# Value blocks of the image normalised before their projection, and the first two images' statistics chains in another order

## The reference, cut to what matters

```python
x = x + gate * _gn(x)        # gate: one number per image and channel
# gate = sigmoid(w_deform . sampled(pooled) + b), pooled = mean over pixels of _gn(x),
# sampled at i + k - 1 + conv3(pooled), clipped, with linear interpolation
y = _gn(x)                   # of the new x
value = conv1x1(y, v_w, v_b)                     # 64 channels
keyf, query = proj(y, k...), proj(y, q...)       # two 1x1 convs with batch norm and relu
# 27 neighbours of each pixel: 3 x 3 at distances 1, 2 and 4; outside the image: zero
sim = softmax(sum_c(query * unfold(keyf)), axis=neighbours)
x = x + conv1x1(sum(sim * unfold(value)), w_w, w_b)
```

## Time and profile before

| | before |
|---|---|
| median of 3 runs | 1502.79 us (1501.54 to 1503.92) |
| profiled execution, its own time | 1504.14 us |
| its span | 1502.4 us |
| TensorE busy | 1452.5 us, 97% |
| VectorE busy | 1240.1 us, 83% |
| ScalarE busy | 1163.9 us, 77% |
| GpSimd busy | 824.5 us, 55% |
| chain that ended last | PE 94%, POOL 2%, issue 2%, DVE 1%, ACT 1% |
| load of an image, 1568 KB | 6.6 us from issue to landing (median) |

### The profile page before, as it was taken

The page is one execution under the profiler, slowest core; times in us unless marked ns, Lnnn a source line. Parts: engine busy times, 40 slices in busy tenths (PEclk is TensorE's granted clock), DMA queues, the critical chain, the costliest instruction groups (busy, mean ns, idle before and its releaser), DMA issues.

```text
span 1502.4 us, 35364 instructions
## 1 busy us (share of the span) xinstructions
PE 1452.5 (97%) x9159; PEld 1189.1 (79%) x9159; DVE 1240.1 (83%) x4631; ACT 1163.9 (77%) x3044; POOL 824.5 (55%) x2313
## 2 busy tenths in 40 slices
PE   1799999999999999999999999999999999999998
PEld 0588888888888888888888888888888888888886
DVE  6488888888888888888888888888888888888876
ACT  2487787887787887787887787887787887787876
POOL 5645565654565654565655565654565655565620
PEclk9999999999999999999999999999999999999999
DMA  2244544454543454544454543454544455543344
GB/s 92 77 123 149 166 111 119 145 166 149 165 116 115 145 166 149 165 106 125 145 166 149 167 115 115 144 166 150 166 107 124 144 166 150 163 123 112 101 122 142
DMA packets 104708, 205.97 MB, mean 137 GB/s; under 512 B 13632, under 2 KB 83776, under 8 KB 96448
## 3 DMA queue, kind: packets, MB, share of 16 engines
q1 hardware_dynamic: 103632, 203.49, 45.8%
q10 hardware_dynamic: 880, 0.23, 0.1%
HBM read 51.62 MB, written 51.38 MB: 69 GB/s over the span
## 4 chain that ended last, share of the span: by engine, by line
PE 94%; POOL 2%; issue 2%; DVE 1%; ACT 1%; ACTq 0%; POOLq 0%; DVEq 0%
PE ps_s L432 23%; PE ps_o L465 20%; PE ps_v L505 12%; PE ps_t L444 11%; PE ps_p L487 11%; PE ps_p L482 11%; PE ps_o L470 3%; PE ps_v L521 1%; PE ps_v L533 1%; PE ps_v L525 1%; POOL hats L767 0%; PE ps_v L528 0%; ACTq L585 0%; POOL xb L836 0%; PE ps_v L532 0%
## 5 line engine op out<-in xcount | busy, mean ns | idle before, releaser
L597 ACT ACTIVATE e<-e,zmin 128x256 f32<-128x256 f32 x800 | 402.8, 503 | 125.0 <-DVE zmin L969 120.4
L969 DVE CUSTOM_DVE_ANT_0 e<-ps_s,mask 128x256 f32<-128x256 f32 x800 | 338.3, 423 | 175.4 <-PE ps_s L432 166.3
L465 PEld LDWEIGHTS ps_o<-eT,v 128*128 128x128 f32 x2688 | 380.3, 191 | 85.3 <-issue 81.6
L465 PE MATMUL ps_o<-eT,v 128*128 128x128 f32 x2688 | 433.4, 276 | 0.1
L432 PE MATMUL ps_s<-kk,qq 128*128 128x256 f32 x1408 | 425.2, 384 | 0.1
L444 PE MATMUL ps_t<-ident,e 128*128 128x128 f32 x1600 | 305.7, 273 | 0.0
L612 ACT ACTIVATE eT<-ps_t 128x512 f32<-128x512 f32 (+1 forms) x416 | 235.7, 567 | 78.2 <-PE ps_t L444 75.8
L444 PEld LDWEIGHTS ps_t<-ident,e 128*128 128x128 f32 x1600 | 225.2, 141 | 80.5 <-issue 0.2
L432 PEld LDWEIGHTS ps_s<-kk,qq 128*128 128x128 f32 x1408 | 223.6, 192 | 47.7 <-issue 41.2
L986 DVE SCALAR_TENSOR_TENSOR e<-e,rz,keep 128x256 f32<-128x256 f32 x480 | 246.0, 513 | 17.1
L505 PE MATMUL ps_v<-wvox,xb 128*128 128x128 f32 x1600 | 219.9, 278 | 0.9 <-DVE v L1007 0.8
(11 more groups left out here) (150 smaller groups left out, 1809.8 us busy)
## 6 DMA issues: line engine op xcount, KB each, us to landing
out_dram<-raw SPq DMA_DIRECT2D x32, 1568.0 KB, 5.7
raw<-in_x_dram SPq DMA_DIRECT2D x31, 1568.0 KB, 6.6
v<-v SPq DMA_DIRECT2D x192, 224.0 KB, 2.9
kk<-kk SPq DMA_DIRECT2D x192, 112.0 KB, 2.2
ksp<-kk SPq DMA_DIRECT2D x192, 64.0 KB, 2.1
v<-v_last SPq DMA_DIRECT2D x64, 128.0 KB, 2.9
kk<-kk SPq DMA_DIRECT2D x32, 224.0 KB, 2.9
v<-v_last SPq DMA_DIRECT2D x64, 96.0 KB, 2.7
```

What stands on the lines that cost most here:

```text
L465: last = nc.tensor.matmul(o[:, UPIX * (u - 1):UPIX * (u + 1)], v[:, s, u, :], eT[:, UPIX * (base + 2 * u - 1):UPIX * (base + 2 * u + 1)], ...
L597: nc.scalar.activation(e[:, i, :], e[:, i, :], ACT.Exp, bias=zmin[:, i:i + 1], scale=-1.0, accum_out=zs[:, i:i + 1]).then_inc(e_done.next( ...
L969: nc.vector.tensor_tensor_reduce(e[:, i, :], ps_s[(TILES * n.parity() + t) % 2][:, 0:KEYS], mask[:].rearrange("p s h a b -> p (s h a b)"), ...
```

## The change

- **Blocks normalised.** `spread` writes `xb` = raw * `Y_A` + `Y_B` with `tensor_scalar` (two scalars per partition) where it copied. The value matmuls take the constant `wvoT`, VectorE adds the constant `wobv`. `yb_row`, `wvox`, `bias`, the second matmul of c6 and step 16 of VectorE's chain go. `spread` of block 0 waits for p11.
- **Shorter chain steps.** Pairs of GpSimd steps become one with two scalars (rsqrt, `diag`, the new moments): p3 writes also `ROOT` = variance * rsqrt, and d7 computes `RG` = 1 / ((1 + EX) * ROOT), so p7 starts with the mean of the new x, and its moments are ready with the fourth step, not the seventh. GpSimd's chain has 32 counts (40 before), VectorE's 15 (16).
- **Image 0 and 1.** Image 0's hats: ScalarE also does three `Relu`, VectorE weighs and adds them (GpSimd's eight steps are only counted). d6 of image 0 moves from slot 25 to 22. Image 1's d6 to pw move later (25..32 to 29..34), its statistics to the slots behind image 0's d9. Image 0's first three strips of projections come 3, 3 and 2 slots earlier. The load of image 2 is issued 19 slots earlier.
- **Tables.** `mask_tables` becomes `distances` (slot 21), `crosses` (behind d7) and `mask_table` (behind image 1's `aggr`). The 19 memsets of `keep` and the wait for the zero fill move behind image 0's p3 (`borders`).
- **All images:** `queries` of strips 0, 2, 3 and 6 one slot later; TensorE's `hidden` no longer waits for `b1x`, ScalarE's does.
- **Dummy matmuls** of 384 columns into `ps_s[0]`: nine behind image 0's c3, five behind its c4.

```diff
+QUERIES_LATER = (0, 2, 3, 6)
+FIRST_UP = (3, 3, 2)
+CH_OF = {0: dict(CH, d6=22), 1: dict(CH, d6=29, a6=29, d7=30, p7=30, c4=31, d9=31, p11=33, pw=34)}
+STATS_1 = {4: (0,), 5: (1,), 6: (2,), 8: (3,), 10: (4,), 12: (5, 6)}
+AWAKE = {CH["c3"]: 9, CH["c4"]: 5}
...
-                        if t == LOAD and (n + 3).exists():
+                        if t == (LOAD if n.offset != -1 else 0) and (n + 3).exists():
...
-                                                    wvox[:, m.parity(), :], start=True, stop=True)
+                                                    wvoT[:], start=True, stop=True)
...
-                            nc.tensor.matmul(ps_v[:, 0:1], w1T[:], col(Y_B + m.parity()), start=True, stop=True)
-                            nc.tensor.matmul(ps_v[:, P:2 * P], yb_row[:], wvoT[:], start=True,
+                            nc.tensor.matmul(ps_v[:, 0:1], w1T[:], col(Y_B + m.parity()), start=True,
                                              stop=True).then_inc(cg.next(), 1)
...
+                    def awake(count):
+                        for _ in range(count):
+                            nc.tensor.matmul(ps_s[0][:, 0:TAPS * P], ident[:], band[:].rearrange("p a b -> p (a b)"),
+                                             start=True, stop=True)
...
+                                if rel == at + (2 if g in QUERIES_LATER else 1):
                                     queries(m, g)
...
+                                for k in range(TAPS) if m.offset == 0 else ():
+                                    act.wait_ge(ag.sem, ag.count(m, k + 1))
+                                    nc.scalar.activation(hats[:, k, 1, :], hats[:, k, 0, :], ACT.Relu, bias=ones[:, 0:1],
+                                                         scale=-1.0).then_inc(a_hats, 1)
...
-                                  lambda: gp.tensor_tensor(col(RG), col(R), col(GATE), ALU.mult),
-                                  lambda: gp.tensor_tensor(col(T0), col(RG), col(D), ALU.mult),
-                                  lambda: gp.tensor_tensor(moment(of_x1, MEAN), col(T0), moment(of_x, MEAN), ALU.add),
+                                  lambda: gp.tensor_scalar(moment(of_x1, MEAN), col(D), col(RG), moment(of_x, MEAN),
+                                                           ALU.mult, ALU.add),
...
-                                  lambda: gp.tensor_tensor(col(T0), a, a, ALU.mult),
-                                  lambda: gp.tensor_tensor(moment(of_x1, VAR), col(T0), moment(of_x, VAR), ALU.mult),
+                                  lambda: gp.tensor_scalar(moment(of_x1, VAR), moment(of_x, VAR), a, a, ALU.mult,
+                                                           ALU.mult),
...
-                                  lambda: gp.tensor_scalar(yb_row[:], ones[:], col(Y_B + i), None, ALU.mult),
-                                  lambda: gp.tensor_scalar(w1x[:, i, :], w1T[:], col(Y_A + i), None, ALU.mult),
-                                  lambda: gp.tensor_scalar(wvox[:, i, :], wvoT[:], col(Y_A + i), None, ALU.mult))
+                            steps(31, lambda: gp.tensor_scalar(w1x[:, i, :], w1T[:], col(Y_A + i), None, ALU.mult))
...
+                            gp.wait_ge(pg.sem, pg.count(m, 31))
...
-                            gp.tensor_copy(to[:, 0, 0:HALO, cs], rows[:, H - HALO:H, at])
-                            gp.tensor_copy(to[:, 0, HALO:SIDE, cs], rows[:, 0:HALO, at])
-                            last = gp.tensor_copy(to[:, 1:CHUNKS, :, cs], rows[:, HALO:H - HALO, at].rearrange(
-                                "p (n r) c -> p n r c", r=SIDE))
+                            for k, rs, src in ((0, slice(0, HALO), rows[:, H - HALO:H, at]),
+                                               (0, slice(HALO, SIDE), rows[:, 0:HALO, at]),
+                                               (slice(1, CHUNKS), slice(0, SIDE), rows[:, HALO:H - HALO, at].rearrange(
+                                                   "p (n r) c -> p n r c", r=SIDE))):
+                                last = gp.tensor_scalar(to[:, k, rs, cs], src, col(Y_A + m.parity()),
+                                                        col(Y_B + m.parity()), ALU.mult, ALU.add)
...
-                                                bias[:, m.parity(), :].unsqueeze(1).to_broadcast([P, last - first, P]),
+                                                wobv[:].unsqueeze(1).to_broadcast([P, last - first, P]),
...
+                        if at == ch(m)["p4"] and m.offset == 0:
+                            dve.wait_ge(pg.sem, pg.count(m, 9))
+                            dve.wait_ge(a_hats, 1)
+                            nc.vector.tensor_scalar(hat_sum[:], hats[:, 0, 1, :], wg_s[:, 9:10], None,
+                                                    ALU.mult).then_inc(pg.sem, 1)
...
-                            step(11, nc.vector.tensor_scalar(col(EX), col(EX), 1.0, None, ALU.add))
-                            step(12, nc.vector.reciprocal(col(GATE), col(EX)))
+                            step(11, nc.vector.scalar_tensor_tensor(col(EX), col(EX), 1.0, col(ROOT), ALU.add, ALU.mult))
+                            step(12, nc.vector.reciprocal(col(RG), col(EX)))
```

More of the change, by code:

```diff
@@ L57 @@
 PIECES = 4
[L59 to L63, removed]
+AWAKE = {CH["c3"]: 9, CH["c4"]: 5}
+CHAIN_READS = ((2, "d1"), (4, "d4"), (13, "d9"), (15, "d13"))
+N_DG, N_PG, N_CG, N_AG = 15, 32, 4, 4
 def half_tile(h):
@@ L146, in end_part, with g_slots, ch @@
         self.here = 0
+def g_slots(m):
+    return [at - (FIRST_UP[g] if m.offset == 0 and g < len(FIRST_UP) else 0) for g, at in enumerate(G_SLOT)]
+def ch(m):
+    return CH_OF.get(m.offset, CH)
 def lagged(n, t, lag):
@@ L712, in _, with borders @@
                     gp.memset(zs[:], 1.0).then_inc(g_zs, 1)
[L713 to L726 removed]
+                    def borders():
+                        gp.wait_ge(v_zero, 3)
+                        cut = 0
+                        for k, kind in enumerate(KINDS):
+                            parts = slice(0, HD)
+                            for part in kind:
+                                if part == "lower":
+                                    parts = slice(HD, P)
+                                    continue
+                                s_at, h_at, rs, cs = part
+                                gp.memset(keep[parts, k, :].rearrange("p (s h r c) -> p s h r c", s=2, h=2, c=SIDE)[
+                                    :, s_at, h_at, rs, cs], 0.0).then_inc(g_keep, 1)
+                                cut += 1
+                                gp.wait_ge(g_keep, cut)
+                        gp.wait_ge(a_zero, 3)
                     def chain(m, at):
@@ L842, in slot @@
                             chain(m, at)
+                        if n.offset == first + 1 and t == CH["p3"] + 1:
+                            borders()
                         for m, rel in items_at(n, t):
@@ L934, in tables @@
                         if t == CH["d4"] + 1:
[L935 removed]
+                            distances()
                         if t == CH["c1"]:
@@ L1015, in step @@
                             dve.wait_ge(dg.sem, dg.count(m, k))
-                        for u in STATS.get(at, ()):
+                        for u in (STATS_1 if m.offset == 1 else STATS).get(at, ()):
                             if u == (2 * (PIECES - 1) if m.offset == 0 else 0):
@@ L1065, in chain @@
                                                              bn_t[:, 0:1], ALU.add))
-                            step(16, nc.vector.tensor_tensor(bias[:, m.parity(), :], ps_v[:, P:2 * P], wobv[:],
-                                                             ALU.add))
                     def slot(n, t):
@@ L1071, in slot @@
                             tables(t)
+                        if n.offset == -1 and t == CH["d7"] - TILES + 1:
+                            crosses()
+                        if n.offset == -1 and t == CH["d13"] - TILES + 2:
+                            mask_table()
                         if n.exists():
```

149 lines of the change are left out of this document (72 added, 77 removed).

## The result

| | before | after |
|---|---|---|
| median of 4 runs each | 1502.2 us (1501.54 to 1503.92) | 1491.67 us (1490.16 to 1492.69) |
| ratio, 95% interval | | 0.9926 [0.9914, 0.9938] |
| profiled execution; its span | 1504.14; 1502.4 us | 1492.62; 1490.9 us |
| c6 of image 0, of image 1, of image 31 (start on TensorE) | 36.8, 81.4, 1433.1 us | 30.4, 70.7, 1420.9 us |
| one image, c6 to c6, median of the images from 1 on | 45.01 us | 44.97 us |

The change is a gain of 0.74%, 10.5 us, where 21.5 was forecast. The time is 6.2 us above the forecast's range (1478 to 1485.5) and 1.7 above the one for 8 in 10 (1490). The two places named in the prediction give the split at once: the period is 44.97, above the mark of 44.95 from which I called the steady part wrong, and the values of b = 4 come at 54.86, just inside the mark of 55.

A forecast was written before the change was run, and what follows sets the result against it. TensorE's queue was taken to bound the steady part, the statistics chains of images 0 and 1 the start. 1502.79 - 12.5 (start) - 9.0 (steady: -7.1 - 6.6 + 3.7 + 1.0) = 1481.3 us; range 1478 to 1485.5, 8 in 10 1475.5 to 1490.

The forecast's parts named there:

- c6's second matmul: TensorE's queue, steady part: removing this narrow matmul saves 0.23 us an image, -7.1 us over 31 images.
- c1: TensorE's weight load no longer waits for GpSimd's `of_x` once `bias` goes: -0.22 x 30 = -6.6 us; bounds 0 and -6.6.
- the cost at c4: Dearer GpSimd block writes, less a shorter p7, make TensorE wait 0.12 us an image: +3.7 us (0 to +18).
- a longer stop at c4: Rival: 0.3 to 0.6 us an image through contention of GpSimd with VectorE, 1487 to 1496 us; chance 0.12.
- a stop of 0.8 us and a time of 1502: Rival of about no change: six block writes 0.25 us dearer each, stop at c4 costing 25 us in all; chance 0.02.
- Queries: ScalarE's queries one slot later; strip 6 delays the next `hidden` by 0.03 us an image: +1.0 us.
- The start: Up to about 66 us, the statistics chains of images 0 and 1 shorten: -12.5 us (-8 to -15).
- Legs 1 and 2: Start, image 0: p1 2.2 us earlier, `Abs` ending at 20.0; then d6 at 22.7, 2.7 us after `Abs`.
- Leg 3: Start, d6 to c4 of image 0: 3.3 us, less 0.6 for p7, so c4 at 25.5.
- Leg 6: Start, `hidden` to image 1's `Abs`: 12.3 us, was 14.1, with TensorE at 2.4 GHz and three strips moved up; `Abs` at 42.6.
- The clock rival: TensorE's clock falls in the start: at 1.2 GHz from 30 to 45 us, +6, or 1487 us; chance 0.18.
- Leg 7: Start, image 1's `Abs` to values of b = 4: 8.8 us, was 11.7, including 0.8 added for blocks; values at 51.4.

The follow-up runs named there:

- e4: Kernel before without c6's second matmul and VectorE's bias step, values getting constant wobv: 1488.72 us, ratio 0.9902.
- e8: Changed kernel with all queries back in their old slot, one after hidden: 1489.2 us, ratio 0.991.
- e7: Changed kernel with chains, hats, tables, dummies and strips of the first two images as before: 1504.62 us, ratio 1.0007.
- e3: Changed kernel with c4 and d9 of images 2 to 31 two slots later: 1472.61 us, ratio 0.9796.
- e1: Changed kernel with blocks 4 and 5 written four slots earlier, ahead of the hats, in all images: 1479.71 us, ratio 0.9843.

## Why the prediction was wrong

**The two bounds and the leaving work were read right.** TensorE's queue sets the steady part, the chain sets the start. c6's second matmul was -0.23 an image and measured 0.23; c1 was -0.22 and measured 0.30. My "next late is then nothing" held too: e4 runs to 44.48. These two gave 16 us by the period, 14.7 by the medians of e4, where I had 13.7.

**The term that failed is the cost at c4.** I had +0.12 an image, 3.7 us; measured 0.6, some 18 us. That is the rival "a longer stop at c4" at its upper end (0.3 to 0.6 us), to which I had given a chance of 0.12, but with contention of GpSimd and VectorE as its cause, and the cause was another. It has four parts.
- The writes: six at +0.15 were to make +0.9; they made +1.09. By mean duration each was near the estimate: 128x384 went from 542 to 680 ns, +0.14, and 128x32 from 281 and 220 ns (the copies L834 and L835) to 423, +0.14 and +0.20. But an instruction overlaps the next, so durations are not what the queue loses. Where VectorE does little, six copies took 1.56 us (44.03 to 45.59 in before, VectorE idle) and six writes 2.68 (38.78 to 41.46 in the changed kernel, VectorE busy for half of it): +1.12, or 0.19 each. Ahead of c4 both are longer, 2.0 and 3.1, with VectorE at work all along. This 0.4 may be contention, but before had it as well; what the change added is GpSimd's own price.
- p7 gave 0.55, where I had 0.6.
- 0.9 less 0.6 is 0.3, and I wrote 0.2. Measured it is 0.54, with 0.06 more before the blocks: 10.40 against 9.80.
- I shifted GpSimd's end against a TensorE that stayed. But the 0.53 that I took out at c6 and c1 lie on TensorE between c6 and c4: the context matmul ahead of c4 comes 0.54 sooner after c6 (28.68 us and not 29.22). The first hat came only 0.43 sooner (19.10 us after c6, it was 19.53), so 0.11 went this way, which is more than the slack of 0.10.

Together: 0.60 later and 0.11 sooner, less 0.10 of slack, is 0.61, and 0.61 was measured. I had 0.2 less 0.10 and took 0.12. And the bracket of the matmul row, 0.36, is not what the queue lost: the weight load stood for 0.52, and the stop cost 0.61. (The upper end of my steady sum was wrong too: c1 at its bound of 0, c4 at +18 and the queries at +4.5 make +15, where I wrote +6.)

By the Trainium skill (GPSIMD Engine Reference, section Elementwise) I had weighed a stop of 0.8 us and a time of 1502. Its figure of about 2.6 cycles an element is too dear for the long write (680 ns, not 830), as I held against it. It was also the wrong figure: the section gives it for `tensor_tensor` with two tensor inputs, and these writes have one. From 128x32 to 128x384 the mean rises by 257 ns, 0.73 ns an element, and 423 ns are there at 32 columns already. That the stop came nearer to 0.8 than to 0.12 was no merit of that rule.

**Queries.** +1.0 us forecast, 2.5 measured (1491.67 against 1489.2 of e8, two sessions) and 3 by the period. The account of one image is then: c6 -0.23, c1 -0.30, g = 6 +0.10, the context matmul at 24 us -0.10, the stop at c4 +0.6 and the eight value matmuls behind it -0.08 (0.89 for 0.97): about zero, where the medians give -0.04.

**The start** was to give 12.5 us (14.2 by its legs, less 1.7 held back). It gave 10.7 at c6 of image 1 (11.5 against e7). So of the 11.0 us that are missing, the steady part has 7.5 and the start 1.8; the rest lies behind the last c6 and between profiled runs and medians. By legs:

| | forecast | measured |
|---|---|---|
| d6 of image 0 | 22.7 | 22.93 |
| c4 | 25.5 | 26.54 |
| first `hidden` | 30.3 | 31.11 |
| `Abs` of image 1 | 42.6 | 45.16 |
| values of b = 4 | 51.4 | 54.86 |

Legs 1 and 2 were right to 0.2. Leg 3 was short by 0.8, 0.54 of it in two steps of p7 that took 0.73 and 0.55 here (L809, L811) and 0.34 and 0.40 in the image shown above. VectorE's `crosses` (24.04 to 25.75), which the change put there, ran beside them. Leg 6 took 14.05 for 12.3. The clock rival explains 0.7 of it: granted clock 0.50 from 35.5 to 38.9 us, and 13.36 in e3 where it was 1.00. The rest is TensorE waiting for `qq` and `v` between the first strips (0.88, 0.65), which "string together" had left out. Leg 7 took 9.70 for 8.8, the dearer writes again (3.21; the copies had taken 1.73 there, and I had added 0.8). The rival put its +6 on a TensorE slow from 30 to 45 us; it was slow for 3.4 of these.

**What I did not ask** is whether the writes have to stand where they stand. I costed them in place, at the two places where they hurt. Ahead of the hats GpSimd waits for ScalarE for 6.79 us in every image, and that row was in the trace of before as well (8.03 us there).

## What to carry to other kernels

- When an edit takes work off the bounding engine and puts work on a helper, compute the helper's slack again after both: TensorE came earlier by what was saved, GpSimd later by what was added, and 0.10 us of slack became a stop of 0.6. Here the whole gain of 16 us went into it, and a move of c4 by two slots brought back 19.
- Cost an instruction by what its queue loses, from one start to the next, and not by its duration. By durations a write was 0.14 to 0.20 us dearer than a copy, by the queue 0.19 for every one of the six.
- Put a helper's added work where it waits anyway, even if that is far ahead of its use, and test the two ends of a late hand-over apart: earlier producer 12 us, later consumer 19, both (with g = 6 put back) 25.5. Then look where the sum comes from: of the last 6.5 us, g = 6 gives 3 and the start 3.5, and in the steady part the two ends cured one and the same stop.

## What the runs showed of the hardware that I had not expected

- A GpSimd `tensor_scalar` of 128x32 with two scalars per partition took 423 ns on average (366 to 432 by kernel) where a copy took 217 to 281. Of 128x128, one scalar and one operation took 617 ns (`diag` before), two scalars and two operations 453 (`diag` after).
- A wait of TensorE for a narrow matmul costs its queue 0.09 us more than the weight load's idle time: 0.29 for 0.21 at c1, 0.61 for 0.52 at c4. After the wait the next score starts 0.23 behind the narrow matmul and not 0.14.
- VectorE's scaling of 128x256 took 0.48 us at most places and 0.74 in e1 at 542.40, its squares of 128x4 0.49 and not 0.16, each time with GpSimd's `shifted` running beside it (542.15 to 543.72). These squares (L1103) took 556 ns on average in the changed kernel and 195 in before (L1058), but 0.16 us in every image of e3, where d9 stands two slots later. That the two engines share something is likely by this, but no run took it apart.
- TensorE's pace at 35.5 us in the start was 1.02 us a `hidden` in some executions (granted clock 1.00) and up to 1.86 in others (0.50 from 35.5 to 38.9), after the same work. What decides it stays open; it is worth about 0.5 us of 1490.
